# Source rows of layer one: 12 of the 49 row blocks made on GpSimd, 37 on VectorE and ScalarE

## The reference, cut to what matters

```python
def _gcn_conv(x, W, b, src, dst, n):
    h = x @ W
    ...
    dinv = jnp.where(deg > 0, jax.lax.rsqrt(deg), 0.0)
    norm = dinv[src_sl] * dinv[dst_sl]
    msgs = h[src_sl] * norm[:, None]
    out = jax.ops.segment_sum(msgs, dst_sl, num_segments=n)
    return out + b
...
h = jax.nn.relu(_gcn_conv(layernorm(x), W1, b1, src, dst, 6250))
h = jax.nn.relu(_gcn_conv(h, W2, b2, src, dst, 6250))
x = x + h
x = x + ffn(layernorm(x))      # 8 experts, top 2, hidden 1024
```

## Time and profile before

| | |
|---|---|
| median of 3 runs | 2028.27 us (2027.53 to 2028.29) |
| the profiled execution | 2047.49 us, of which the span is 2045.8 |
| TensorE busy | 1867.4 us (91%) |
| VectorE busy | 1345.9 us (66%) |
| GpSimd busy | 1146.3 us (56%) |
| ScalarE busy | 729.1 us (36%) |
| mean granted clock of TensorE | 0.966 of full speed |

### The profile page before, as it was taken

The page is one execution under the profiler, slowest core; times in us unless marked ns, Lnnn a source line. Parts: engine busy times, 40 slices in busy tenths (PEclk is TensorE's granted clock), DMA queues, the critical chain, the costliest instruction groups (busy, mean ns, idle before and its releaser), DMA issues. The chain is left out here.

```text
span 2045.8 us, 40624 instructions
## 1 busy us (share of the span) xinstructions
PE 1867.4 (91%) x13425; PEld 1222.5 (60%) x13426; DVE 1345.9 (66%) x3357; ACT 729.1 (36%) x1669; POOL 1146.3 (56%) x1208
## 2 busy tenths in 40 slices
PE   3679999999999998999999999935999999999997
PEld 2545555455555553544444444414989989989996
DVE  6585676676676662566676767567666676666664
ACT  3664444444444440111111111112444444444442
POOL 6215666566676644667666766302566565555553
PEclk8899999999999999999999999965999999999998
DMA  8264455455555437778877887724233322233322
GB/s 282 75 221 167 170 174 188 167 175 191 178 175 175 172 142 269 250 268 269 268 251 266 293 296 255 283 89 179 43 48 50 52 49 45 49 49 48 50 45 27
DMA packets 126408, 329.39 MB, mean 161 GB/s; under 512 B 20736, under 2 KB 80000, under 8 KB 119360
## 3 DMA queue, kind: packets, MB, share of 16 engines
q0 software_dynamic: 59072, 142.05, 26.2%
q1 hardware_dynamic: 47376, 167.36, 22.9%
q10 hardware_dynamic: 19824, 18.23, 2.8%
HBM read 214.10 MB, written 113.45 MB: 160 GB/s over the span
## 5 line engine op out<-in xcount | busy, mean ns | idle before, releaser
L943 PE MATMUL mp_o<-rows,m_counts 128*128 128x512 f16 x1960 | 490.3, 381 | 8.5 <-ACT m_counts L1073 8.5
L585 POOL DMA_INDIRECT m_x_t<-rows_d,take_src x311 | 366.5, 1178 | 204.0 <-PE mp_x L956 155.6
L1889 PE MATMUL rp_o<-rows,adj_ring 128*128 128x512 f16 x1960 | 455.9, 380 | 8.9 <-issue 8.9
L1816 POOL DMA_INDIRECT r_took<-rows_d,take_src x311 | 324.2, 1043 | 178.9 <-PE rp_g L1905 106.2
L1073 ACT ACTIVATE m_counts<-mp 128x490 f16<-128x490 f32 (+4 forms) x544 | 292.1, 559 | 351.9 <-PE mp L972 284.8
L1889 PEld LDWEIGHTS rp_o<-rows,adj_ring 128*128 128x128 f16 x1960 | 191.9, 98 | 225.9 <-issue 11.2
L2447 PE MATMUL fp_h<-f_xt,w 128*128 128x256 f16 x2688 | 305.1, 274 | 0.3 <-issue 0.3
L2466 PE MATMUL fp_y<-w,f_hh 128*128 x2688 | 302.4, 273 | 0.0
L943 PEld LDWEIGHTS mp_o<-rows,m_counts 128*128 128x128 f16 x1960 | 182.8, 98 | 185.2 <-issue 11.6
L2447 PEld LDWEIGHTS fp_h<-f_xt,w 128*128 x2688 | 264.3, 98 | 31.6 <-issue 0.7
L2466 PEld LDWEIGHTS fp_y<-w,f_hh 128*128 128x128 f16 x2688 | 263.0, 98 | 30.4
(11 more groups left out here) (257 smaller groups left out, 1913.0 us busy)
## 6 DMA issues: line engine op xcount, KB each, us to landing
adj<-m_counts SPq DMA_DIRECT2D x40, 1568.0 KB
adj_ring<-adj SPq DMA_DIRECT2D x40, 800.0 KB
adj_ring<-adj SPq DMA_DIRECT2D x40, 768.0 KB
r_raw<-in_L_ffn_W_dram POOLq DMA_DIRECT2D x16, 1024.0 KB
w_parts<-r_parts POOLq DMA_DIRECT2D x8, 1024.0 KB
w<-w_parts SPq DMA_DIRECT2D x4, 2048.0 KB
rows<-in_x_dram SPq DMA_DIRECT2D x7, 896.0 KB, 8.5
rows_d<-rows SPq DMA_DIRECT2D x7, 896.0 KB, 4.7
```

The costliest lines, as they stand in the source:

```text
L585: pool.indirect_dma_start(out=took[:, r, :], out_offset=None, in_=k.rows_d[0], in_offset=bass.IndirectOffsetOnAxis(ap=k.take_src[:, i:i + ...
L943: mm = nc.tensor.matmul(ps_o[q], counts[:, q, s, :], k.rows[0][:, s, :], start=i == 0, stop=i == BLOCKS - 1)
L1816: pool.indirect_dma_start(out=took[:, r, :], out_offset=None, in_=k.rows_d[1], in_offset=bass.IndirectOffsetOnAxis(ap=k.take_src[:, i:i + ...
L1889: mm = nc.tensor.matmul(ps_o[b % 2], adj[:, m % ADJ_RING, at:at + P], rows[:, s, :], start=s == 0, stop=s == BLOCKS - 1)
```

## The change

Blocks 21 to 32, the last twelve early ones (`POOL_ROWS`), are taken from ScalarE and VectorE. GpSimd makes both halves of each with three instructions: it scales the product in place, copies it to fp16 as the high half, and subtracts for the low half. It does so ahead of everything else in its part of the steps, from the moment the scales are there. The 21 early blocks that are left (`KEPT_ROWS`) are spread over the same 16 steps. In the first destination block's sum the twelve come behind all others, and SP's stores wait for them by a semaphore of their own.

```diff
@@ -106,6 +106,8 @@
 XW_LAST = XW_FIRST + (COLS - 1) * XW_EACH
 LATE = BLOCKS - XW_LAST
 LOW_LATER = 2
+POOL_ROWS = list(range(XW_LAST - 12, XW_LAST))
+KEPT_ROWS = XW_LAST - len(POOL_ROWS)
 COL_BLOCKS = P * SPAN // P
 PARTS = 5
 ROW = D + EXPERTS
@@ -238,7 +240,7 @@
 
     if n < 1 or n > LATE:
         return []
-    first, end = ((n + i) * XW_LAST // LATE for i in (-1, 0))
+    first, end = ((n + i) * KEPT_ROWS // LATE for i in (-1, 0))
     return [*range(first, end), XW_LAST + n - 1]
 
 
@@ -440,6 +442,7 @@
              "w_summed", "w_ready", "xw", "xw_ready"))
         valued, starts_sum, starts_ready, taken_in, take_ready, take_hot, take_used, rows0_out = (sem("m_" + x) for x in (
             "valued", "starts_sum", "starts", "taken_in", "take", "take_hot", "take_used", "rows0_out"))
+        pool_hi, pool_lo = sem("m_pool_hi"), sem("m_pool_lo")
         took_in = [sem(f"m_took{r}") for r in range(TAKE_RING)]
         xt_in = [sem(f"m_xt_in{r}") for r in range(XT_RING)]
         x_in = [sem(f"m_x_in{g}") for g in range(X_LOADS)]
@@ -512,7 +515,12 @@
             def together():
                 n = BLOCKS // X_LOADS
                 for g in range(X_LOADS):
-                    sp.wait_ge(lo_done, max(ROW_PLACE[r] for r in range(g * n, (g + 1) * n)) + 1)
+                    kept = [ROW_PLACE[r] + 1 for r in range(g * n, (g + 1) * n) if r in ROW_PLACE]
+                    pooled = [r - KEPT_ROWS + 1 for r in range(g * n, (g + 1) * n) if r in POOL_ROWS]
+                    if kept:
+                        sp.wait_ge(lo_done, max(kept))
+                    if pooled:
+                        sp.wait_ge(pool_lo, max(pooled))
                     sp.dma_start(k.rows_d[0][g * n * P:(g + 1) * n * P, :].rearrange("(b p) d -> p b d", p=P),
                                  k.rows[0][:, g * n:(g + 1) * n, :]).then_inc(rows0_out, 16)
                 for n in range(STEPS):
@@ -585,9 +593,23 @@
                 pool.indirect_dma_start(out=took[:, r, :], out_offset=None, in_=k.rows_d[0],
                                         in_offset=bass.IndirectOffsetOnAxis(ap=k.take_src[:, i:i + 1], axis=0)).then_inc(took_in[r], 16)
 
+            def rows_of(b):
+
+                i = b - KEPT_ROWS
+                nc.gpsimd.tensor_scalar(xs[:, b, :], xs[:, b, :], scale_in[:, b:b + 1], None, ALU.mult).then_inc(pool_hi, 1)
+                pool.wait_ge(pool_hi, 2 * i + 1)
+                nc.gpsimd.tensor_copy(k.rows[0][:, b, 0:D], xs[:, b, :]).then_inc(pool_hi, 1)
+                pool.wait_ge(pool_hi, 2 * i + 2)
+                nc.gpsimd.tensor_tensor(k.rows[0][:, b, D:2 * D], xs[:, b, :], k.rows[0][:, b, 0:D],
+                                        ALU.subtract).then_inc(pool_lo, 1)
+
             def together():
                 takes = iter(range(len(TAKES)))
                 i = next(takes)
+                pool.wait_ge(dinv_ready, 1)
+                pool.wait_ge(xw_ready, XW_LAST)
+                for b in POOL_ROWS:
+                    rows_of(b)
                 for n in range(STEPS):
                     for b in range(DENSE):
                         if LAST[b] + 1 == n:
@@ -928,14 +950,18 @@
             def sum_part(b, part, parts):
 
                 q = b % 2
-                order = [s for s in ROW_ORDER if s != b] + [b]
+                order = [s for s in ROW_ORDER + POOL_ROWS if s != b] + [b]
                 if part == 0:
                     if b >= 2:
                         pe.wait_ge(agg_ready, PLACE[b - 2] + 1)
                     pe.wait_ge(emptied, LAST[b] + 1)
                 if b == 0:
 
-                    pe.wait_ge(lo_done, ROW_PLACE[order[(part + 1) * BLOCKS // parts - 1]] + 1 if part < parts - 1 else BLOCKS)
+                    used = order[part * BLOCKS // parts:(part + 1) * BLOCKS // parts]
+                    pe.wait_ge(lo_done, max([ROW_PLACE[s] + 1 for s in used if s in ROW_PLACE], default=1))
+                    if any(s in POOL_ROWS for s in used):
+                        pe.wait_ge(lo_done, len(ROW_ORDER))
+                        pe.wait_ge(pool_lo, max(s - KEPT_ROWS + 1 for s in used if s in POOL_ROWS))
                 for i in range(part * BLOCKS // parts, (part + 1) * BLOCKS // parts):
                     s = order[i]
                     if s == b:
```

## The result

The changed kernel takes 2032.74 us (median of 20 runs, 2029.52 to 2038.64) where the kernel before, run beside it, takes 2027.22 (20 runs, 2019.54 to 2034.71): ratio 1.0029, 95% interval 1.0021 to 1.0038, that is 5.9 us slower (5.5 by the two medians). Forecast were 5.7 us, 2034.0 in all.

What follows compares the result with a forecast made beforehand. VectorE bounds the row making; TensorE's restart hangs on count block 0's store. Last early low 130.28 - 4.7 + 4.8 = 130.4; plus 13.78 + 5.6 gives 149.8 against 144.09, 5.7 us later: 2034.0 us, range 2028 to 2042.

Steps and rivals of the forecast that it cites:

- Moved stores: SP's store queue: group 2 waits for the last early low, so five groups precede the count block, not three: 5.6 us.
- The clock after the restart: TensorE's restart: idle stretch grows to some 11 us, but nothing charged, as the clock had fallen before too.
- What it does to VectorE: Making of the rows: GpSimd's reads take turns with one-hots and early lows, costing VectorE 4.8 us, ends 0 and 11.5.
- Removed work: Making of the rows: twelve low halves leave VectorE, 4.7 us; ScalarE's twelve high halves are worth nothing more.
- Added work on GpSimd: From the ready scales on: 36 GpSimd instructions, alone about 23 us.
- GpSimd's own end: Twelfth block on GpSimd done at about 130 to 133, hidden before group 4's store turn at 136.7.
- VectorE waits for whole GpSimd instructions: Rival, making of the rows: two thirds of 18 us, 12, lost; restart 12.9 us later, 2041; chance 0.15.
- No slower: Rival: GpSimd's reads find free turns, stall near 0, only 0.9 us left, 2029.2; decided at 3.2 us stall; chance 0.28.
- GpSimd ends last: Rival: GpSimd's 36 instructions end at 144, after group 4's turn; restart 13.7 us later, 2042; chance 0.12.
- faster: Rival: TensorE's restart would have to come at 140.0, needing DMA at 480 GB/s against 330; chance 0.03.

Runs made afterwards that it cites:

- The fourth experiment: Kernel before, SP's stores in the order they get done and count block 0 stored ahead of the last two row groups: 2020.21 us, ratio 0.9965.

## Why the prediction was right

The mechanism held: the stores made most of the loss, and VectorE lost about what it had saved. That the number came within 0.2 us of 5.9 was also luck, as the paragraph on the clock shows.

**Moved stores: right in place and size.** Forecast were five group stores in a row from the last early low on, 19.4 us from the first issue to ScalarE, and 5.6 us for the two groups. Measured are five in a row, 19.52 us, and 5.74. The DMA of the changed kernel from 114 to 126 us has no pause (packets, MB and share of the engines):

```profile
DMA packets 4068, 4.19 MB, mean 349 GB/s; under 512 B 71, under 2 KB 4060, under 8 KB 4060
...
q1 hardware_dynamic: 4067, 4.17, 105.1%
```

With the stores ordered by when they are complete, 4.5 of the 5.9 us went (ratio 1.0007 for 1.0029).

**The clock after the restart: a term put at nothing.** The prediction charged nothing for the longer idle time, since the clock had fallen in the old one too. The granted clock was 0.50, its lower level, for the first 2.6 us after the restart before and for the first 5.4 us after the change. One of ScalarE's copies some 35 us behind the restart, at 179.82 before and 168.09 after, starts 7.7 us later from S, where the restart was 6.5 us later: 1.2 us more. Then 1.7 us come back. From S + 105 to S + 125 the trace of before has a granted clock of 0.91; the trace after has none of that dip in the same work, 7.7 us later (times from the span's start, before and after):

```profile
202.10:222.10 20.00, 17.56 (x128) 9.23 (x125) 11.22 (x15) 8.10 (x16) 10.77 (x10) 0.91 0.41 142
```

```profile
190.40:210.40 20.00, 17.56 (x139) 9.55 (x136) 12.63 (x17) 8.85 (x17) 12.06 (x11) 1.00 0.44 147
```

Behind it a copy at 230.51 before starts at 217.11 after, 6.0 us later from S. So 6.5 at the restart, 1.2 and -1.7 make the 6.0, and the last two were in no sum; that they nearly cancel is luck. Why the dip is missing after the change is open: it is missing in the run without reads too, and there in the other five traces.

**What it does to VectorE: right.** The groups of VectorE from S to the last early low after the change, and the same groups before:

```profile
L780 DVE SCALAR_TENSOR_TENSOR rows<-rows,m_scale_in,rows 128x256 f16<-128x256 f32 x21 | 12.6, 617 | 1.2 <-ACT rows L1115 1.1
L842 DVE TENSOR_TENSOR m_oh_lane<-lane_b,m_edge_lane 128x1920 f16<-128x1920 bf16 x6 | 7.2, 1203 | 0.0
L842 DVE TENSOR_TENSOR m_oh_cell<-m_cells,m_edge_cell 128x1470 f16<-128x1470 bf16 x6 | 6.9, 1158 | 0.0
L780 DVE SCALAR_TENSOR_TENSOR rows<-mp_x,m_scale_in,rows 128x256 f16<-128x256 f32 x11 | 5.2, 473 | 0.0
```

```profile
L758 DVE SCALAR_TENSOR_TENSOR rows<-rows,m_scale_in,rows 128x256 f16<-128x256 f32 x33 | 14.3, 473 | 0.8 <-ACT rows L1089 0.8
L820 DVE TENSOR_TENSOR m_oh_lane<-lane_b,m_edge_lane 128x1920 f16<-128x1920 bf16 x6 | 6.9, 1145 | 0.0
L820 DVE TENSOR_TENSOR m_oh_cell<-m_cells,m_edge_cell 128x1470 f16<-128x1470 bf16 x6 | 5.5, 912 | 0.0
L758 DVE SCALAR_TENSOR_TENSOR rows<-mp_x,m_scale_in,rows 128x256 f16<-128x256 f32 x11 | 5.2, 472 | 0.0
```

Early lows lost 144 ns each, the two one-hots 58 and 246, the late lows 1: 21 x 0.144 + 6 x 0.058 + 6 x 0.246 = 4.85 us. Forecast were 4.8, and nothing for the late lows, whose first input is in PSUM. The waits for ScalarE, 0.3 us more, were not in the sum. The number was luckier than its working. It was a layout by hand of one period, and the work added alone cost 6.9 us at the low: what a block costs VectorE (0.40 us here, 0.58 there) depends on which instruction GpSimd happens to meet. The layout let GpSimd in when the running VectorE instruction ends; in the work added alone it waited through two. The price by the reads, 0.24 + 0.24 + 0.48 = 0.96 us where a block takes turns, was of the right kind: in the work added alone the three meetings with an early low cost 0.22 + 0.13 + 0.41 = 0.76.

**Removed work: right.** 33.16 - 4.7 + 4.85 + 0.3 = 33.6, measured 33.90. The run without reads agrees: 28.5 + 0.83 (the two lengthened instructions) + 0.6 (ScalarE) is 29.9; measured 30.24, with some 8 ns on each low. (The fourth experiment, where GpSimd does none of this work, has these 8 ns too, so they are not the memsets'.)

**Added work on GpSimd: two prices right, one too small, one too large.** Its groups from S to 114 us after the change:

```profile
L599 POOL TENSOR_SCALAR rows<-rows,m_scale_in 128x256 f32<-128x256 f32 x12 | 13.6, 1133 | 11.7 <-DVE dinv_in L853 11.7
L603 POOL TENSOR_TENSOR rows<-rows,rows 128x256 f16<-128x256 f32 x12 | 12.9, 1075 | 1.0
L601 POOL CAST rows<-rows 128x256 f16<-128x256 f32 x12 | 7.9, 655 | 0.8
```

The shortest cast took 0.40 us and the shortest two-input one 0.72, for 0.42 and 0.68 forecast. The product with the scale, forecast at 0.42, took 0.92 at the least, and 0.96 the first time, before any wait. So the slope of the select was the wrong row for it. The waits between a block's instructions, forecast at 0.4 us a block, took 0.15 (1.0 + 0.8 us for twelve). So 36 instructions alone are some 27 us, not 23.

**GpSimd's own end: hidden, by less than forecast.** The twelfth block was done at 112.34 + 1.45 = 113.79, S + 36.07; the forecast was S + 33 to 36, and it would have counted from S + 39.6. The forecast's range was too narrow for its own rate: at five instructions in 5.5 us, its slow end, 36 take 39.6 us. Six in 5.7 us came. Group 4's store was issued right behind that block, before its turn in the burst.

**The rivals.** "VectorE waits for whole GpSimd instructions": refuted as it was priced. GpSimd's undisturbed time is 12 x (0.96 + 0.40 + 0.72) = 25 us; VectorE lost 4.85, and 6.9 where the work was added alone. Nor did a single meeting with an early low cost a whole instruction: 0.41 us of 0.72 was the most, as the added work showed. (The one-hot that lost 0.41 to an add of 0.43 remains the row nearest to this rival.) One stretch of the changed kernel's timeline:

```profile
97.69 1.11 DVE L842 TENSOR_TENSOR m_oh_cell<-m_cells,m_edge_cell 128x1470 f16<-128x1470 bf16 x1
...
98.11 1.22 POOL L603 TENSOR_TENSOR rows<-rows,rows 128x256 f16<-128x256 f32 x1
...
98.73 0.89 DVE L780 SCALAR_TENSOR_TENSOR rows<-rows,m_scale_in,rows 128x256 f16<-128x256 f32 x1
```

The two-input instruction at 98.11 took 1.22 us for its 0.72, the one-hot running then 1.11 for 0.91, and the low behind it 0.89 for 0.47: both sides gave something up. The Trainium skill (SBUF — State Buffer, section "Who interferes with whom") gives the shared ports to whichever engine issues first and has the other blocked until that instruction ends. The full spans, which the prediction charged to VectorE by it, would need GpSimd to be first each time. On who interferes the rows agree with the page (early lows 473 to 617 ns, late lows 472 to 473); on the price they do not: a block cost VectorE 0.40 us here, where it takes GpSimd 2.1. "No slower" fell with the stall of 4.85 against its 3.2; "GpSimd ends last" with the end at S + 36.07; "faster" with the DMA at 320 to 349 GB/s.

## What to carry to other kernels

When work is moved, look at what it completes and what is queued behind that: this change left the bounding engine where it was but for 0.74 us, yet cost 5.9 us, mostly because one store of seven now waits for the last step, with four groups and a count block in line behind it. The same look finds a gain: the count block taken out of that line makes the kernel before 7 to 8 us faster, more than the 4.7 us that the shift takes off VectorE. A longer wait of TensorE can also cost behind its end: look at the granted clock of the first microseconds after it, not only at the mean. An idle engine that reads the memory of the busy one is not free; its price is set by which instructions meet, so measure it with the work added alone and also with the work moved, and take neither for the other.

## What the runs showed of the hardware

GpSimd's memsets, which read nothing, lengthened VectorE's int32 copy from 0.31 to 0.72 us and its 9-column `tensor_scalar` from 0.16 to 0.58, but not its two-input instructions: they ran for the first 6 us after S, and the one-hots and the early low beside them took 1.16, 0.92 and 0.48 us, as before. With GpSimd's reading instructions the two-input ones grew. Beside GpSimd's product with the scale the same `tensor_scalar` took 0.17 us and the copy 0.31; but beside a cast, in the kernel with the work added, the copy took 0.49. And the burden can fall on either side: beside an unrelieved VectorE GpSimd's two-input instruction took up to 2.48 us for its 0.72, waiting through two one-hots that kept their 1.14 and 0.91. What a wait of TensorE costs shows in part behind its end: in the 10 us after it went on, the granted clock was 1.00 where it had stood 0.5 us, 0.83 where it had stood 2.4, 0.87 for 5.9 and 0.73 for 11.5.
